# A post-norm decoder layer: the beginning rebuilt and attention's slots in another order

## The reference

```python
x = layernorm(x + attn(x))        # 16 heads of 8; q, k, v and the output are circulant products plus a bias
x = layernorm(x + xattn(x, ctx))  # similarity of x with 120 context rows, two softmaxes, (4D x D) product
x = layernorm(x + ffn(x))         # 8 experts, top 2 by softmax(x @ gate_w.T) + gate_b, and a shared expert
```

## Time and profile before

| what | us |
|---|---|
| median of 3 runs | 437.2 (435.69 to 444.21) |
| the profiled execution | 439.32 |
| its span, first to last instruction | 437.6 |
| PE busy | 355.7 (81%) |
| DVE busy | 280.9 (64%) |
| POOL busy | 192.0 (44%) |
| ACT busy | 175.9 (40%) |

### The profile page before, as it was taken

One profiled execution on the slowest core, in us unless ns is written; L12 is line 12 of the kernel. 1 busy time (PEld: TensorE's weight loads), 2 busy tenths in 40 slices (PEclk: granted clock), 3 DMA queues, 4 the chain that ended last, 5 costly groups with the idle time before them and its releaser, 6 DMA issues.

```text
span 437.6 us, 8506 instructions
## 1 busy us (share of the span) xinstructions
PE 355.7 (81%) x2402; PEld 231.0 (53%) x2415; DVE 280.9 (64%) x834; ACT 175.9 (40%) x498; POOL 192.0 (44%) x377
## 2 busy tenths in 40 slices
PE   2638588878987986987998599887989999999791
PEld 1223356656654764766667455444445555555450
DVE  3424257656877767686876876788566666666422
ACT  1211224433543432334444244434455556555404
POOL 9700014312211366531662344436775666656323
PEclk9999969979988788896989779999999999999896
DMA  4763734575617523130112000102211111110063
GB/s 100 167 184 94 214 90 111 181 225 153 186 66 219 181 81 87 32 103 28 41 52 97 2 18 18 50 13 79 76 54 50 45 44 44 42 45 30 19 199 96
DMA packets 53197, 39.56 MB, mean 90 GB/s; under 512 B 7623, under 2 KB 46632, under 8 KB 53147
## 3 DMA queue, kind: packets, MB, share of 16 engines
q1 hardware_dynamic: 50881, 34.33, 28.1%
q0 software_dynamic: 2272, 4.69, 3.2%
HBM read 26.05 MB, written 12.69 MB: 89 GB/s over the span
## 4 chain that ended last, share of the span: by engine, by line
PE 45%; DVE 23%; issue 8%; DMA 6%; POOL 6%; SPq 5%; ACT 5%; another core or an unknown queue 2%; ACTq 0%; POOLq 0%; DVEq 0%
PE pT L1468 6%; PE pS L1468 6%; PE pM L1479 3%; DVE negmax L921 3%; PE pM L1276 2%; PE pT L1445 2%; PE pT L1300 2%; PE pO L1459 2%; DVE PT L1052 2%; POOL rstd L602 2%; PE pS L1290 2%; PE pO L1313 2%; DMA X<-in_x 2%; PE pS L1469 1%
## 5 line engine op out<-in xcount | busy, mean ns | idle before, releaser
L700 POOL DMA_INDIRECT ys<-sim_rhs,row_dest x39 | 40.7, 1045 | 41.7 <-ACT sim_rhs L855 39.9
L921 DVE TENSOR_REDUCE negmax<-pS 128x4 f32<-128x512 f32 x64 | 43.2, 679 | 19.5 <-PE pS L1290 19.3
L755 ACT ACTIVATE PT<-pT 128x512 f32<-128x512 f32 x64 | 38.1, 595 | 43.9 <-PE pT L1300 43.0
L1290 PE MATMUL pS<-Kdiag,Qst 128*128 128x512 f32 x64 | 42.8, 678 | 13.4 <-DMA Qst<-parts_scr 12.9
L1468 PE MATMUL pT<-W,XH 128*128 (+1 forms) x94 | 51.1, 625 | 0.2 <-issue 0.2
L1468 PE MATMUL pS<-W,XH 128*128 (+1 forms) x94 | 49.0, 603 | 0.0
L1052 DVE TENSOR_TENSOR PT<-pT,PT 128x512 f32<-128x512 f32 x47 | 32.4, 690 | 24.6 <-PE pT L1469 11.4
L600 POOL TENSOR_SCALAR vareps<-meanvar 128x1 f32<-128x1 f32 x32 | 7.3, 227 | 88.9 <-DVE meanvar L950 88.7
L839 ACT COPY XH<-pO 128x384 f32<-128x384 f32 x47 | 22.5, 479 | 48.1 <-PE pO L1461 42.2
L1479 PEld LDWEIGHTS pM<-W,XH 128*128 128x128 f32 x188 | 28.0, 191 | 21.2 <-issue 17.5
L622 POOL DMA_INDIRECT xs<-X,slot x32 | 33.5, 1045 | 8.3 <-issue 6.0
(11 more groups left out here) (264 smaller groups left out, 834.0 us busy)
## 6 DMA issues: line engine op xcount, KB each, us to landing
parts_scr<-qk_hi SPq DMA_DIRECT2D x16, 256.0 KB, 2.9
W<-in_L_ffn_w SPq DMA_DIRECT2D x16, 256.0 KB, 3.2
Kdiag<-parts_scr SPq DMA_DIRECT2D x64, 48.0 KB
Qst<-parts_scr SPq DMA_DIRECT2D x32, 96.0 KB
Kst<-parts_scr SPq DMA_DIRECT2D x32, 96.0 KB
Qdiag<-parts_scr SPq DMA_DIRECT2D x64, 48.0 KB
sim_add<-xs SPq DMA_DIRECT2D x39, 65.0 KB
parts_scr<-qk_lo SPq DMA_DIRECT2D x8, 256.0 KB, 3.4
```

Source lines behind the costliest of these rows:

```text
L700: pool.indirect_dma_start(ys.ap(), bass.IndirectOffsetOnAxis(ap=row_dest[:, k:k + 1], axis=0), YO[:, i % RING, :], None).then_inc(s_ysc[i ...
L755: act.activation(PT[:, u % 3, :], pT[:, 0, :], ACT.Exp, scale=SCALE).then_inc(p_sb, 1)
L921: dve.tensor_reduce(out=negmax[:, b % 2, HG * j:HG * (j + 1)], in_=pS[:, u % 2, :].rearrange("p (g k) -> p g k", g=HG), axis=AX.X, op=ALU.max,
L1290: pe.matmul(pS[:, u % 2, :], Qst[:, (b // 2) % 2, j, (b % 2) * P:(b % 2 + 1) * P], Kdiag[:, b % 2, j, :, :], start=True, stop=True).then_i ...
```

## The change

- **Circulants in two halves.** Those of queries and keys are written, read and turned first, those of values and output afterwards. The keys of group 0 go to a bank of pT, so that they need not wait for pM.
- **Bias rows by a product.** The four bias rows are loaded as one row on one partition and spread over the partitions by a product with ones into pX; ACT copies them to `wide_rows`.
- **Context spread.** Context is loaded in four parts at slots -4, 7, 19, 35 and transposed (through pM) at slots 0, 10, 26, 42.
- **Unread products.** TensorE multiplies ones with ones into pO: 10, 6, 2 and 30 products in the beginning (before the transposes of X, after them, beside the copy of the circulants, and after the bias rows), 2 in each slot from -7 to -1, and 4 in slot 0. Nothing reads them.
- **Slots.** The group steps are at offsets -4, -2, 2 instead of -4, -3, 0, and step 0 comes at the start of its slot; spills at -1 and 3 instead of -2 and 1, and later than `max_rows` in a slot; `q_stack` three slots earlier, `k_stack` one earlier. X of group 1 is loaded in the beginning. The counts of groups 0 and 1 come in step 13 instead of 7, and their scatter six slots later. The shared expert takes 20 slots instead of 18, the down product comes 4 slots after the last up product instead of 2, and the last three DVE operations of each half go one slot later. The bias loads are spread, the gate weights go to slot 3, and the last two experts' up weights are loaded at slots 67 and 68 and awaited from tile 8.

The core of the diff (the new functions in full):

```diff
-GROUP_STEPS = {-4: 0, -3: 1, 0: 2}
+GROUP_STEPS = {-4: 0, -2: 1, 2: 2}
+SPILL_SLOTS = (-1, 3)
...
-PREP_SLOT = -11
-X_SLOTS = {-7: 1, 1: 2, 9: 3}
-SHARED_SLOT, SHARED_SLOTS = 25, 18
+GATE_SLOT = 3
+CONTEXT_SLOT = -6
+CONTEXT_LOADS = {-4: 0, 7: 1, 19: 2, 35: 3}
+X_SLOTS = {1: 2, 9: 3}
+BIAS_SLOTS = {7: 0, 11: 1, 15: 2}
+SHARED_SLOT, SHARED_SLOTS, SHARED_DOWN = 25, 20, 9
...
-COUNT_STEP, ROUTE_STEPS = 7, 10
-HALVE_SLOTS = {14: E, **{36 + e: e for e in range(E)}}
-UP_SLOTS = {**{15 + 4 * e: e for e in range(E - 2)}, 62: E - 2, 63: E - 1}
-DOWN_SLOTS = {13 + 4 * k: (2 * k, 2 * k + 1) for k in range(E // 2)}
+LATE_COUNT, COUNT_STEP = 7, 13
+ROUTE_STEPS = 10
+HALVE_SLOTS = {22: E, **{36 + e: e for e in range(E)}}
+UP_SLOTS = {**{15 + 4 * e: e for e in range(E - 2)}, 67: E - 2, 68: E - 1}
+DOWN_SLOTS = {17 + 4 * k: (2 * k, 2 * k + 1) for k in range(E // 2)}
 ROUTE_SLOT = 25
-SCATTER_SLOT = ROUTE_SLOT + ROUTE_STEPS
 FFN_SLOT = 67
+WARM_UP, WARM_CIRC, WARM_COPY, WARM_STACKS, WARM_SCORES, WARM_MAX = 10, 6, 2, 30, 2, 4
...
+        def context_step(n):
+
+            q, r = divmod(n - CONTEXT_SLOT, G4 * U)
+            return 0 if n == 0 else q if r == 0 and 1 <= q < NG else None
+
+        def count_step(g):
+            return COUNT_STEP if g < NG - 2 else LATE_COUNT
+
+        def scatter_slot(g):
+            return G4 * U * g + ROUTE_SLOT + count_step(g) + 3
+
+        def projection_bank(g, k):
+
+            return pT[:, 0, :] if (g, k) == (0, 2) else pM[:]
...
-            return (g, i // 2) if 0 <= g < SG and i % 2 == 0 else None
+            if not 0 <= g < SG or i % 2 or i == 16:
+                return None
+            return (g, 8) if i == 2 * SHARED_DOWN else (g, i // 2)
...
-            sp.wait_ge(s_circw, 64)
-            sp.dma_start(hankel, bass.AP(circ_scr, 1, [[1, P], [2 * D, 4], [1, D]])).then_inc(s_circ, 16)
-            sp.dma_start(ctx_sb[1:NC1], ctx_1024.rearrange("b j d -> j b d")).then_inc(s_ctx, 16)
-            sp.wait_ge(c_zero, 2)
...
+            circ_source(2, wv_c)
+            circ_source(3, wo_c)
+            circ_read(0)
+            circ_read(1)
+            sp.wait_ge(c_zero, 3)
+            small = [(one_row[:, D * k:D * k + r.shape[0]], r.rearrange("(o n) -> o n", o=1)) for k, r in enumerate((wv_b, wo_b, b_qv, gate_b))]
...
                 sp.dma_start(to, src).then_inc(s_small, 16)
+            load_x(1)
...
+                if n >= -3 and n % U == 1 and (n + 3) // U < B:
+                    max_rows((n + 3) // U)
                 for g in range(NG):
-                    if n == G4 * U * (g - 1) - 2:
-                        spill(g, 0)
-                    if n == G4 * U * (g - 1) + 1:
-                        spill(g, 1)
+                    for i, at in enumerate(SPILL_SLOTS):
+                        if n == G4 * U * (g - 1) + at:
+                            spill(g, i)
+                if n % (2 * U) == 3 and 0 <= (n + 13) // (2 * U) < B // 2:
+                    q_stack((n + 13) // (2 * U))
+                if n % U == 2 and 0 <= (n + 10) // U < B:
+                    k_diag((n + 10) // U)
+                if n % (2 * U) == 7 and 0 <= (n + 9) // (2 * U) < B // 2:
+                    k_stack((n + 9) // (2 * U))
+                if n % U == 0 and 0 <= n // U + 1 < B:
+                    q_diag(n // U + 1)
                 if n in X_SLOTS:
                     load_x(X_SLOTS[n])
-                if n >= -3 and n % U == 1 and (n + 3) // U < B:
-                    max_rows((n + 3) // U)
-                if n % U == 2 and 0 <= (n + 10) // U < B:
-                    k_diag((n + 10) // U)
-                if n % (2 * U) == 6 and 0 <= (n + 10) // (2 * U) < B // 2:
-                    q_stack((n + 10) // (2 * U))
-                if n % (2 * U) == 0 and 0 <= n // (2 * U) + 1 < B // 2:
-                    k_stack(n // (2 * U) + 1)
-                if n % U == 0 and 0 <= n // U + 1 < B:
-                    q_diag(n // U + 1)
...
+                if n in CONTEXT_LOADS:
+                    q = CONTEXT_LOADS[n]
+                    sp.dma_start(ctx_sb[1:NC1, G4 * q:G4 * q + G4, :],
+                                 ctx_1024[G4 * q:G4 * q + G4].rearrange("b j d -> j b d")).then_inc(s_x[q], 16)
...
-                if n == 11:
                     up_weights(E, s_w_shared)
                     down_weights(E, s_w_shared)
                 if n in UP_SLOTS:
-                    if n >= SHARED_SLOT + SHARED_SLOTS * SG:
+                    if UP_SLOTS[n] >= E - 2:
                         sp.wait_ge(f_ps, 9 * SG)
                     up_weights(UP_SLOTS[n], s_w_up if UP_SLOTS[n] < E - 2 else s_w_last)
...
+            pool.memset(ones[:], 1.0).then_inc(c_zero, 1)
+            pool.memset(ident[:], 0.0).then_inc(c_ident, 1)
+            pool.memset(flip, 0.0).then_inc(c_flip, 1)
             pool.memset(bsim[:], 0.0).then_inc(c_zero, 1)
-            pool.memset(ident[:], 0.0).then_inc(c_ident, 1)
-            pool.memset(ctx_sb[0:1], 0.0).then_inc(c_pad, 1)
-            pool.memset(flip, 0.0).then_inc(c_flip, 1)
-            pool.memset(ones[:], 1.0)
...
-                    act.activation(qk_hi[:, i, :], pM[:], ACT.Identity, bias=qk_bias[:, i:i + 1],
+                    act.activation(qk_hi[:, i, :], projection_bank(g, k), ACT.Identity, bias=qk_bias[:, i:i + 1],
                                    scale=1.0).then_inc(hi_sb, 1)
+                    if (g, k) == (0, 2):
+                        act.wait_ge(gwT_ps, 1)
+                        act.copy(wide_rows[:], pX[:, 0, 0:3 * D + E]).then_inc(gwT_sb, 1)
...
             def front(n):
+                if group_step(n) and group_step(n)[1] == 0:
+                    group(*group_step(n))
+                if n == 0:
+                    context(0)
...
+                if n == GATE_SLOT:
+
+                    act.wait_ge(gwT_ps, 2)
                     act.copy(gwT[:], pX[:, 1, 0:E]).then_inc(gwT_sb, 1)
-                    for q in range(4):
-                        context(q)
                 front(n)
+                if context_step(n):
+                    context(context_step(n))
...
+
+            def circulants(half):
+                dve.wait_ge(circ_ps, half + 1)
+                dve.tensor_copy(circ[:, 2 * half:2 * half + 2, :].rearrange("p k n -> p (k n)"), pX[:, half, 0:2 * D]).then_inc(circ_sb, 1)
...
+                if n == 0:
+                    context(0)
...
+
+            def shared_hidden(g, i):
+
+                c, step = i // 4, i % 4
+                done = 9 * g + i
+                if i < 8 and step == 3:
...
+            def warm(n):
+
+                for _ in range(n):
+                    pe.matmul(pO[:, 0:P], ones[:], ones[:], start=True, stop=True)
...
-                projections_free()
+                if (g, k) != (0, 2):
...
+                    if g == 0:
+                        warm(WARM_CIRC)
                 else:
                     if g == 0 and k == 1:
-                        pe.wait_ge(s_circ, 16)
                         pe.wait_ge(c_flip, 2)
-                        pe.matmul(pX[:, 0, :], flip, hankel.rearrange("p k n -> p (k n)"), start=True, stop=True).then_inc(circ_ps, 1)
+                        circulants(0)
+                        warm(WARM_COPY)
                         pe.wait_ge(circ_sb, 1)
                     pe.wait_ge(xT_sb, g + 1)
-                    pe.matmul(pM[:], circ[:, k - 1, :], XT[:, g % 2, :], start=True, stop=True).then_inc(qk_ps, 1)
+                    pe.matmul(projection_bank(g, k), circ[:, k - 1, :], XT[:, g % 2, :], start=True, stop=True).then_inc(qk_ps, 1)
                     issued["qk"] += 1
+                    if (g, k) == (0, 2):
+                        circulants(1)
+                        pe.wait_ge(s_small, 16 * SMALL)
+                        pe.matmul(pX[:, 0, 0:3 * D + E], ones[0:1, :], one_row[:], start=True, stop=True).then_inc(gwT_ps, 1)
+                        warm(WARM_STACKS)
+
+            def circulants(half):
+                pe.wait_ge(s_circ[half], 16)
+                pe.matmul(pX[:, half, 0:2 * D], flip, hankel[:, 2 * half:2 * half + 2, :].rearrange("p k n -> p (k n)"),
+                          start=True, stop=True).then_inc(circ_ps, 1)
+
+            def context(q):
+                projections_free()
+                if q == 0:
+                    pe.wait_ge(c_pad, 1)
+                    pe.wait_ge(s_small, 16 * SMALL)
+                pe.wait_ge(s_x[q], 32)
+                for c in range(G4):
+                    mm = pe.transpose(pM[:, c * NC1:(c + 1) * NC1], ctx_sb[:, G4 * q + c, :], ident[0:NC1, 0:NC1])
+                mm.then_inc(cT_ps, 1)
+                issued["t"] += 1
...
+                if group_step(n) and group_step(n)[1] == 0:
+                    group(*group_step(n))
+                if n == 0:
+                    context(0)
                 if 0 <= n + LEAD < U * B:
                     scores(n + LEAD)
+                    if n < 0:
+                        warm(WARM_SCORES)
```

(26 more changed lines are left out.)

109 lines of the change are left out of this document (58 added, 51 removed).

## The result

| | median us | lowest to highest | runs |
|---|---|---|---|
| kernel before | 436.44 | 434.05 to 444.21 | 4 |
| changed kernel | 423.25 | 422.4 to 424.71 | 4 |

The ratio is 0.972, with a 95% interval from 0.966 to 0.978: 13 us faster, where 26 were forecast. The profiled execution of the changed kernel took 423.84, its span is 422.1 and its mean granted clock 0.951 (before: 437.6 and 0.925).

A forecast was written before the change was run, and what follows sets the result against it. Slots were taken as a loop through several engines, none full, with 41 us lost at a few stops and the clock falling behind them. Terms summed to -29.3, +3.3 for unnamed stretches, -26: 411 us from 437.2, range 401 to 425.

The forecast's parts named there:

- three signs: Forecast wrong if slot 0 starts after 36, slots 0 to 63 take over 185, or tiles change by more than 3.
- Slots 19 to 28: +0.8, the context's third step: Slots 19 to 28: the context's third step adds 0.8 us.
- Moved issues on SP lie in slots where SP waits for `max_rows`: SP's queue in the slots: moved bias rows, weights and `load_x` fall where SP waits anyway; no term of their own.
- After that SP alone sets slot 0 ... TensorE isn't on that path: Beginning, after the last spill lands: SP's read-backs and context load set slot 0, at 32.8 against 41.34, -8.5 us.
- Slots 48 to 50: Slots 48 to 50: 10.99 falls to 5.5 us as the counts leave, -5.5.
- Slots 41 to 48: Slot 41: 9.73 falls to 5.2 us, -4.5; slots 42 to 48: last context step, +0.8; together -3.7.
- After 63: After slot 63: +1.5 us, as the second down product now lies just ahead of the tiles, whose products stay.
- Unread products: TensorE kept at its upper level, mainly in the beginning; about 3 of the 26 us gain comes from them.
- The stops move: Rival, slots: VectorE is late and other waits replace those removed, middle gains only a quarter; 421 us, chance 0.20.
- The clock stays up: Rival, slots: nearly all of some 45 us at half clock goes, some 10 more gained; 401 us, chance 0.10.
- Only SP's order counts, the beginning is as long as before: Rival, beginning: slot 0 starts where it did, only the middle gains 8.5; about 429 us, chance 0.07.
- Context arrives late: Rival, slots 10, 26, 42 and slot 0's part: TensorE waits for context, ending slower, at 447 us; chance 0.03.

The follow-up runs named there:

- r5: Changed kernel with the counts of groups 0 and 1 back in step 7, scatter back too: 424.6 us, ratio to the kernel before 0.976.
- r6: Changed kernel with the shared expert as before (18 slots, down product two slots after the last up product): 424.54 us, ratio to the kernel before 0.976.
- r7: Changed kernel with group steps, spills and stacks back in their old slots: 427.94 us, ratio to the kernel before 0.986.
- r12: Changed kernel with the context's third load in slot 11 and the up weights of slot 19 in slot 22: 418.56 us, ratio to before 0.942.
- r9: Changed kernel again, unaltered, on a third chip: 423.01 us, ratio to the kernel before 0.953.
- r1: Kernel before with the new order of slots alone; old beginning and context, no unread products: 425.93 us, ratio 0.969.
- r4: Changed kernel without the two unread products in each of slots -7 to -1: 421.62 us, ratio to the kernel before 0.958.
- r11: Changed kernel with 48 unread products after the bias rows instead of 30, none in the slots: 422.51 us, ratio to the kernel before 0.953.
- r10: Changed kernel without any unread product: 425.76 us, ratio to the kernel before 0.959.
- r8: Changed kernel with counts, shared expert and groups all as before, leaving the new beginning, spread context and unread products: 435.88 us, ratio to before 1.003.
- r3: Changed kernel with the context's third load and the up weights of slot 19 both in slot 22: 423.06 us, ratio to the kernel before 0.960.
- r2: Changed kernel with the context's third load in slot 22 instead of 19: 427.07 us, too spread for a ratio.

## Why the prediction was half right

**Direction and place were right.** The stops that the trace of before named went, each where its part of the order had been moved, and each came back when that part was undone (r5, r6, r7). Slot 0, 1 to 16, 28 to 34, 34 to 41 and 50 to 63 lie within about 2 us of their terms. The clock came back as those stops went: from slot 0 to 63 about 14 us are at half clock, where 44 were. By the pair of the earlier trace rows that is worth 15 (an estimate), and the slots are 15.4 shorter. Of the three signs that I had named for a wrong forecast one came: slot 0 starts after 36, at 36.75. The other two didn't (183.5 for 185, tiles longer by 2.4 for 3).

**The step that failed first: "Slots 19 to 28: +0.8, the context's third step"**, and with it "Moved issues on SP lie in slots where SP waits for `max_rows`". I priced moved issues by whether SP had time for them. In this slot it had not, since SP came to the maxima 3.6 late, and above all they took the DMA engines' time. The earlier trace rows had the warning: slots 16 to 19 were at 0.76 and 19 to 28 at 0.61 busy. The keys' spill moved two slots later and `q_stack` three earlier, so both fell together with 752 KB of context and weights (240 + 2 x 256) in front of 8 KB writes that TensorE needs some two slots later. The term was +0.8 and measured +8.3, of which r12 shows 4.7 to be the pile (30.0 to 25.3; 31.4 to 25.3 beside r9). Of the other 3.7 to the old 21.6, r1, which has neither the context nor its loads in the slots, has 2.4 as well; those I haven't taken apart.

**The second: "After that SP alone sets slot 0 ... TensorE isn't on that path".** The forecast of the last spill (15.4 to 16.8) and of the first scores (23 to 25) held: 15.27 and 23.86. From there SP was not alone. The last spill took 5.42 to land where I took 2.9 to 3.2 from a median, with the reads of the query stack issued beside it at 16.57. TensorE had finished the 30 products at 19.75 and waited 4.12, the clock fell, and early scores with their two unread products came every 1.27. The maxima were issued at 31.33 instead of 27.1 to 28.5. Then queries, values and context handed pM from one to the next until 35.9, and slot 0 came at 36.75, 5.4 behind the maxima where I had 5.1. So the miss of 3.9 lies nearly all ahead of the maxima: SP was through with its read-backs at 29.4, one to two late by the slow landing, and then waited 1.9 more for TensorE's scores. So the end of the beginning is a loop of TensorE, VectorE and SP in which no one part is alone on the path: r4 shortened one part, r11 another, and each ran into the next.

**The sizes.** Slots 48 to 50: 3.5 gained of 5.5, since a stop of 4.6 stays in slot 48. Slots 41 to 48: 2.6 of 3.7, as slot 42 now takes 6.2. After 63: +4.4 for +1.5; the second down product costs 1.7 as said, the tiles are 2.4 longer, in part by the clock behind an old stop. I had called the tiles untouched, but the same stop there has the clock fall behind it in one trace and not in the other.

**Unread products.** The sum had about 3 from them. All of them together are worth 2.7 (r10 against r9). "TensorE: Matmul & The Clock Gate" of the Trainium skill, Part 1, puts the ramp's penalty at under 1% of a typical span. By that rule, this agrees: 2.7 is 0.6% of 423, and up to slot 0 it is 0.5. The loss behind stops in mid-kernel is another and larger matter here, as the 44 and 14 us at half clock show. But not each wait brings the half rate back, as the prediction had put it: after the 2.54 in the tiles of before it stayed up, and slots 50 to 63 of the changed kernel hold 6.65 us of idle time at a clock of 1.00.

**The rivals.** *The stops move* gave 421, near the measured 423, and it was partly right. It had VectorE late and other waits in place of those removed, and these came: 9.8 in 13 waits for `X`, where 2.0 in 4 were before. But they are short, and with them the slots are still 15.4 shorter; the stop that cost eight is a DMA's. *The clock stays up* was right on the mechanism for 30 of its 45 us at half clock, but that was no gain on top of the forecast, it was the gain itself. *Only SP's order counts, the beginning is as long as before*: slot 0 did come earlier, and yet r8 says that the new beginning without the new order is worth nothing (1.003 [1.000, 1.007]). It had the right account in the wrong place. With the new order it is worth some: on the first chip r3 and r4 are 2.9 and 4.3 below r1 (r3 has the weights of slot 19 moved as well). *Context arrives late* had the wrong victim: none of TensorE's long waits in the slots is for context; its load made another transfer late.

**What stays open**: where the beginning's 3 us go under the old order, the long slots 42, 48 and 62, why the clock stays up over the new short waits and fell behind the old ones, why the same issues landed sooner in r1 than in r2, and why the same kernel before differs by 5 us between two sets when the changed one doesn't. That it has more stops behind which the clock can fall is a reason that fits, and only argued.

## What to carry to other kernels

Price a moved DMA not by its queue's free time only, but by all bytes that are under way when the next small, urgent transfer is issued behind it: add them up by slot, and look at the DMA column before moving anything into a busy window (here 0.76 and 0.61). Do not take a stop's length for its price, nor idle time for the measure of the gain: here idle time stayed at 32 to 34 us and the slots became 15 shorter, because the clock no longer fell. Undo each part of a large change by itself: here the new beginning brought nothing without the new order of slots (r8), and one hidden side effect had eaten 4.5 us and could be had back by moving two numbers. And when two kernels differ in how many stops they have, their ratio may vary with the execution (0.972 and 0.953 here), so time them side by side.

## What the runs showed of the hardware that I had not expected

- In the changed kernel an 8 KB write lands 1.8 to 6.6 us after its issue (median 2.1), the longest with the DMA engines 0.97 busy ahead of it.
- A spill of 256 KB with a median of 3.0 to landing took 5.42 as the last of six issued within 4 us, with reads issued just behind it.
- From slot 0 to 63 TensorE was idle for 33.8 us in one kernel and 32.4 in the other, and its mean granted clock was 0.89 in the one and 0.96 in the other: the sum of the waits does not tell what the clock does.
- After a wait of 2.5 on TensorE the clock stayed up in one trace (next pair 1.08, before) and fell in the other (1.93, changed), at the same place of the same work.
- The FFN's tiles, the same instructions in all kernels, took 151.8 to 153.4 in the four traces from one chip, and 154.8 to 158.2 in the others.
